# Two-layer decoder on one core: in the second cross-attention an item's context is weighted in one block of 448 columns, where it was two blocks of 224

## Reference, cut to what matters

```python
def _L1_xattn_ref(x, context, Wq, Wk, Wv, Wo, bo):
    h, C = (8, 128)                                   # 8 heads of 128
    q = (x @ Wq).reshape(B, Tq, h, C) * SCALE
    k = (context @ Wk).reshape(B, Tk, h, C) * SCALE
    v = (context @ Wv).reshape(B, Tk, h, C)
    attn = jax.nn.softmax(jnp.einsum('bqhc,bkhc->bhqk', q, k), axis=-1)
    out = jnp.einsum('bhqk,bkhc->bqhc', attn, v).reshape(B, Tq, h * C)
    return out @ Wo + bo
x = _layernorm(x + _L1_xattn_ref(x, ctx_768, ...))
x = _layernorm(x + _L1_ffn_ref(x, ...))
```

## Time and profile before

| | us |
|---|---|
| median of 3 runs | 1011.96 |
| the profiled execution, its own time | 1011.95 |
| its span, first to last instruction | 1010.1 |
| TensorE busy with products | 965.1 |
| VectorE busy | 575.1 |
| ScalarE busy | 408.1 |
| GpSimd busy | 154.3 |

### The profile page before, as it was taken

How to read it: one execution, slowest core, us unless ns; L and a number is a source line. 1 busy time by engine, 2 the same in 40 slices (tenths; PEclk the granted TensorE clock), 3 DMA queues, 4 the chain that set the end, 5 groups by cost and what they waited for, 6 DMA issues and landing times. The chain is left out here.

```text
span 1010.1 us, 16932 instructions
## 1 busy us (share of the span) xinstructions
PE 965.1 (96%) x6432; PEld 747.1 (74%) x6432; DVE 575.1 (57%) x1307; ACT 408.1 (40%) x1069; POOL 154.3 (15%) x151
## 2 busy tenths in 40 slices
PE   9899799999999999989999999989989999999985
PEld 4678687878778777768999998656666777777663
DVE  3887546555555556566756555358644444555544
ACT  3556434343343333335454544357633232332221
POOL 0323610110110100004443432300010000000000
PEclk9999899999999999989999999989999999999998
DMA  4500100000000000019311000710000000000000
GB/s 158 202 1 1 53 16 1 17 17 1 16 2 1 1 2 1 1 39 290 119 42 49 35 1 21 173 21 2 3 18 17 16 16 16 16 1 25 6 6 18
DMA packets 26824, 36.32 MB, mean 36 GB/s; under 512 B 3648, under 2 KB 22160, under 8 KB 26752
## 3 DMA queue, kind: packets, MB, share of 16 engines
q1 hardware_dynamic: 26752, 35.35, 12.0%
HBM read 30.75 MB, written 2.75 MB: 33 GB/s over the span
## 5 line engine op out<-in xcount | busy, mean ns | idle before, releaser
L1128 ACT ACTIVATE x_prob<-bank,x_negmax 112x375 f32<-112x375 f32 x128 | 72.2, 569 | 144.0 <-DVE x_negmax L1038 144.0
L1847 DVE TENSOR_TENSOR moe_h_low<-moe_sq,moe_h_high 128x512 fp32r<-128x512 f32 (+1 forms) x64 | 54.4, 872 | 53.6 <-ACT moe_h_high L1947 40.9
L1924 POOL TENSOR_TENSOR moe_sq<-moe_r 128x512 f32<-128x512 f32 (+1 forms) x64 | 64.2, 1006 | 105.7 <-ACT moe_r L1956 83.9
L1038 DVE TENSOR_REDUCE x_negmax<-bank 112x1 f32<-112x375 f32 x128 | 64.1, 543 | 9.6 <-PE bank L926 7.3
L1956 ACT ACTIVATE moe_r<-bank 128x512 f32<-128x512 f32 (+1 forms) x64 | 34.9, 546 | 75.7 <-PE bank L101 68.7
L101 PE MATMUL bank<-moe_w_low,moe_h_high 128*128 128x256 f32 x224 | 63.4, 283 | 0.0
L101 PE MATMUL bank<-moe_w_high,moe_h_low 128*128 128x256 f32 x224 | 63.3, 283 | 0.0
L101 PE MATMUL bank<-moe_w_high,moe_h_high 128*128 128x256 f32 x224 | 63.3, 283 | 0.0
L1043 DVE COPY x_prob_t<-bank 125x336 f32<-125x336 f32 x128 | 58.4, 497 | 2.8 <-PE bank L935 1.4
L926 PE MATMUL bank<-x_kt,x_qt 64*112 64x375 f32 x256 | 58.3, 521 | 1.2 <-DVE x_kt L1030 0.7
L935 PEld LDWEIGHTS bank<-const,x_prob 112*125 112x125 f32 x384 | 49.8, 188 | 6.6 <-issue 3.8
(11 more groups left out here) (370 smaller groups left out, 2252.2 us busy)
## 6 DMA issues: line engine op xcount, KB each, us to landing
moe_w<-in_L_ffn_W SPq DMA_DIRECT2D x15, 512.0 KB, 5.0
ctx_t<-in_ctx_t SPq DMA_DIRECT2D x8, 376.0 KB, 4.3
x_ctx_t<-in_ctx_t SPq DMA_DIRECT2D x8, 376.0 KB, 3.2
wk<-in_L_xattn_Wk SPq DMA_DIRECT2D x2, 1024.0 KB, 5.3
wv<-in_L_xattn_Wv SPq DMA_DIRECT2D x2, 1024.0 KB, 8.4
wq<-in_L_xattn_Wq SPq DMA_DIRECT2D x2, 1024.0 KB, 10.5
wo<-in_L_xattn_Wo SPq DMA_DIRECT2D x2, 1024.0 KB, 12.0
xt<-in_xt SPq DMA_DIRECT2D x1, 896.0 KB, 4.7
```

The lines of the kernel that those rows point to most:

```text
L1038: dve.tensor_reduce(negmax[:, g:g + 1], S_BANK(u, e)[0:T, 0:S], AX_X, ALU.max, negate=True).then_inc(max_ready, 1)
L1128: act.activation(PROB(u, e)[:, :], S_BANK(u, e)[0:T, 0:S], ACT.Exp, bias=negmax[:, g:g + 1], accum_out=total[:, g:g + 1]).then_inc(p_ready, 1)
L1847: dve.tensor_tensor(h_low[half][:, m, 0:size], sq[m % 2][:, 0:size], h_high[half][:, m, 0:size].bitcast(F32), ALU.subtract).then_inc(low_d ...
L1924: pool.tensor_tensor(sq[m % 2][:, 0:size], r[m % 2][:, 0:size], r[m % 2][:, 0:size], ALU.mult).then_inc(sq_done, 1)
```

## The change

TensorE weights an item's context once, with all eight heads (448 columns for each e), in unit 0 of the next round, between the EARLY jobs and `turn`. Both calls behind `turn` are gone. VectorE and ScalarE collect a bank whole in unit 0 of the next round, in the place where the second half was collected; the collection in unit 2 is gone. The counts that the semaphores are compared with follow. The jobs and their places stay.

```diff
@@ job
                     elif kind == OUT:
-                        pe.wait_ge(ot_act, 2 * i + 2)
-                        pe.wait_ge(ot_dve, 2 * i + 2)
+                        pe.wait_ge(ot_act, i + 1)
+                        pe.wait_ge(ot_dve, i + 1)
@@ weigh
-                def weigh(i, half):
-                    pe.wait_ge(pt_copied, 2 * (i * J + 2 * half + 2))
-                    wait_past(pe, ot_act, 2 * i + half)
-                    wait_past(pe, ot_dve, 2 * i + half)
-                    if i > 0 and half == 0:
+                def weigh(i):
+                    pe.wait_ge(pt_copied, 2 * (i + 1) * J)
+                    wait_past(pe, ot_act, i)
+                    wait_past(pe, ot_dve, i)
+                    if i > 0:
                         pe.wait_ge(job_used, number[(CTX_MAIN, i)] + 1)
-                    cols, heads, c = slice(half * 2 * T, (half + 1) * 2 * T), slice(2 * half, 2 * half + 2), cn[i % 2]
-                    turned = lambda e, k: pt[e][:, k, heads, :].rearrange("s j t -> s (j t)")
+                    cols, c = slice(0, J * T), cn[i % 2]
+                    turned = lambda e, k: pt[e][:, k, :, :].rearrange("s j t -> s (j t)")
@@ TensorE's order
                         for job_ in jobs(i, u, EARLY):
                             job(job_)
+                        if u == 0 and i > 0:
+                            weigh(i - 1)
                         turn(i, u)
                         for job_ in jobs(i, u, MID):
                             job(job_)
-                        if u == 0 and i > 0:
-                            weigh(i - 1, 1)
-                        if u == 2:
-                            weigh(i, 0)
                         for job_ in jobs(i, u, LATE):
                             job(job_)
                 for job_ in first_left:
                     job(job_)
-                weigh(B - 1, 1)
+                weigh(B - 1)
@@ VectorE (ScalarE alike, with its two copies)
-                def collect(i, half):
-                    cols = slice(half * 2 * T, (half + 1) * 2 * T)
-                    dve.wait_ge(pv_done, 2 * i + half + 1)
-                    if i > 0 and half == 0:
+                def collect(i):
+                    cols = slice(0, J * T)
+                    dve.wait_ge(pv_done, i + 1)
+                    if i > 0:
                         dve.wait_ge(job_ready, number[(OUT, i - 1)] + 1)
-                    dve.tensor_copy(ot[:, 1, 2 * half:2 * half + 2, :], U_BANK[1][:, cols].rearrange("d (j t) -> d j t", j=2)).then_inc(ot_dve, 1)
+                    dve.tensor_copy(ot[:, 1, :, :], U_BANK[1][:, cols].rearrange("d (j t) -> d j t", j=J)).then_inc(ot_dve, 1)
...
                         if u == 0 and i > 0:
-                            collect(i - 1, 1)
+                            collect(i - 1)
...
-                        if u == 2:
-                            collect(i, 0)
```

More of the change, by code:

```diff
@@ L1501, in _ @@
                             residual(i - 1)
-                        if u == 2:
-                            collect(i, 0)
                         if u == 3 and i > 1:
                             base(i - 2)
-                collect(B - 1, 1)
+                collect(B - 1)
                 gates(B - 3)
@@ L1538, in exps, with collect @@
                                        accum_out=total[:, g:g + 1]).then_inc(e_ready, 1)
[L1540 to L1543, removed]
+                def collect(i):
+                    cols = slice(0, J * T)
+                    act.wait_ge(pv_done, i + 1)
+                    if i > 0:
                         act.wait_ge(job_ready, number[(OUT, i - 1)] + 1)
-                    act.copy(ot[:, 0, 2 * half:2 * half + 2, :], U_BANK[0][:, cols].rearrange("d (j t) -> d j t", j=2))
-                    act.copy(ot[:, 2, 2 * half:2 * half + 2, :], U_BANK[2][:, cols].rearrange("d (j t) -> d j t", j=2)).then_inc(ot_act, 1)
+                    act.copy(ot[:, 0, :, :], U_BANK[0][:, cols].rearrange("d (j t) -> d j t", j=J))
+                    act.copy(ot[:, 2, :, :], U_BANK[2][:, cols].rearrange("d (j t) -> d j t", j=J)).then_inc(ot_act, 1)
                 def deviation(i):
```

## The result

The changed kernel takes 1020.56 us in the median of four runs (1017.56 to 1022.33), the kernel before 1012.54 beside it: a ratio of 1.0092 (95% interval 1.0062 to 1.0122), 6 to 12 us slower. Timed again on another chip it was 1.0108 (1.0083 to 1.0133). The direction was forecast; the size was not: 5.9 us were, and 9 came. The median stands just inside the stated range, which went to 1020.6, but the kernel before stood 0.6 higher beside it; on the 1011.95 us of the forecast the ratio gives 1021.3.

The account below looks back on a forecast made before the run. TensorE, busy 96% of the span, was taken to bound the kernel. Steps of -3.6, +1.3, +5.4, +1.9, +0.8 and +0.1 sum to +5.9 on 1011.95, so 1017.8 us; range 1014.4 to 1020.6.

Parts of the forecast that it names:

- Step 1: Weighting: a whole block takes 7.07 us against 7.52 for two halves; 0.45 gained for each of 8 items, -3.6.
- Step 2: Round 0, unit 2: without the half block, the next scores wait for unit 3's exponentials, +1.3 us.
- Step 3: Unit 2, rounds 3 to 7: OUT waits 1.08 us for ScalarE to empty GATES from the job bank, +5.4.
- Step 4: Unit 0, rounds 4 to 6: CTX_REST waits for LOW to be emptied, 0.58 twice and 0.73 in round 6, +1.9 us.
- Step 5: Round 7, unit 0: VectorE's larger collection makes row maxima and the next scores late, +0.8 us.
- Step 6: Tail after round 7: dropped collect(7, 0) saves 0.31 us, the larger last collection costs 0.37; together +0.1.
- rival D: TensorE's clock falls around new 1.1 us idle stretches; one OUT block at 1.2 GHz adds 5.4, 1023.2 us; 4%.
- a clock under 1.00 before 1000 us: Sign of being wrong: in the changed profile, stretches before 1000 us show a granted clock below 1.00.

Follow-up runs that it names:

- GATES alone covered: Changed kernel with only GATES moved between the 128-feature and 64-feature parts of the whole block in unit 0; timed once, 1011.54 us.
- LOW alone covered: Changed kernel with only LOW moved between the whole block and turn, its addition ahead of VectorE's copies; timed once, 1017.96 us.
- both covered: Changed kernel with GATES moved between the whole block's two parts and LOW between block and turn; ratio 1.0031 to the kernel before.

## Why the prediction was wrong in size

- *Step 1, width.* A block's slot is 7.20 in rounds 1 to 5 and 7.11 after, against 7.07; two halves in its place cost 0.39 more and not 0.45. Against the two half blocks of before (7.51) seven items gain 2.35 to the scores of round 7, where 3.15 was forecast. A record takes 0.375, its columns and 0.002. The statement of the Trainium skill ("TensorE: Matmul & The Clock Gate", Back-to-back issue gap) that a sustained product of 512 columns costs about 131 ns, far less than in proportion to 128 columns, is not borne out for the fp32 products here. The same section's formula for a single product, columns by 2.4 GHz plus about 2.5 ns, gives 0.376 for 448 columns if each is counted twice, as these fp32 records ask; no run here has another type.
- *Step 2, round 0.* 1.24 idle for the load, 1.3 from slot to slot: right, and the half block put back gives it back.
- *Step 3, OUT behind GATES.* The slot of GATES is 1.26 where it was 0.18, five waits of 1.08 as forecast, and moving GATES away removes them and 0.4 more from OUT of item 6's delay: right.
- *Step 4, CTX_REST behind LOW.* 1.8 against 1.9: right, except that round 6 has the 0.59 of the others and not 0.73.
- *Step 5, round 7.* The scores of units 2 and 3 stand 4.56 apart where they stood 4.23: 0.3, not 0.8. Counted from `turn`'s slot at 961.11, the collection ends 3.4 later and not 3.6, and the row maxima start 4.17 later and not 4.58, while VectorE had no idle stretch between: each part of its work was a little shorter or overlapped a little more than forecast.
- *Steps 1 to 5 together.* That the scores of round 7 came at +5.4 against +5.2 is partly luck: 0.8 less gain by width and 0.5 less wait in round 7 nearly cancel.
- *Step 6, tail.* `collect(7, 0)` gone: NT 0.38 earlier behind OUT of item 6 (9.32 against 9.70); the last collection 1.03 as worked out. Right in these terms, but this step is where the failure lies. It priced the last block like the others, at 2.4 GHz, and rival D was given only 4%, because idle stretches of 1.24 and 2.58 us had left the clock at 2.4 GHz. In both profiles of the changed kernel the clock falls at that wait, now 2.20 long, for 3.4 us, which costs 1.4; and again ahead of the last BASE and LOW and not behind them, which costs about 1.5 more. With the wait filled both are gone, and 6.1 is left where 5.9 was forecast. The low clock from 980 to 984 is also one of the signs by which the prediction said it would be wrong, a clock under 1.00 before 1000 us.

Why the clock falls at this wait and did not before is open. The stretch of 2.58 was read from a trace in which 3.75 us of dense weighting stood ahead of OUT of item 6; the change lays this work behind the wait and puts a wait of 1.1 in its place. But with GATES alone covered the weighting stands behind the wait too, and the clock stayed up; with both covered no wait of 1.1 is left ahead, and it fell. No run puts dense work back ahead of the wait.

So the missing term is a low clock behind round 7, 2.9 us of 9.1. The range was too narrow at its upper end for the same reason: it held 1 us for the clock in the tail, and the clock costs three times that.

## What to carry to other kernels

A block that hides the emptying of a shared bank is worth its cover, not only its instructions: before merging or moving it, list for each slot it leaves what now follows directly on what, and when the bank between them is free. Here each such wait came within 0.15 us of its forecast, but for that of round 7. The granted clock belongs into the sum wherever TensorE has long waits already: an edit that moves work around such a wait can bring a fall there that the trace of before doesn't show, and a few unread products in the wait are a cheap way to find out what it costs.

## What the runs showed of the hardware

The length of an idle stretch alone does not tell whether the clock falls. One of 2.58 us left it at 2.4 GHz in the kernel before, and one of 2.19 with GATES alone covered; one of 2.20 (from 978.6 to 980.8) let it fall in both profiles of the changed kernel, 1.8 us into the wait, and it fell up to 1.5 us behind the end of the same wait with LOW alone covered, with both covered and with two halves. Twice, with item 0 in two halves, it fell behind a wait of 1.06 that left it up in every other profile. What decides was not found; the runs show that 1.9 us of products in the long wait prevents the fall there.

Fillers in the tail put the fall off in both kernels they were put in: from 258.8 to 265.7 us into the stage in the kernel before, and from 252.0 to 262.3 in the other. Falls ahead of the stage, in code that no version changes, differ in length from one execution to the next: in the two profiles of the changed kernel they sum to 17.1 and 30.7 us, and the stage starts at 738.66 and 744.0. That is 5.3 us apart, more than half of what the change cost.
